# Moving a bias from TensorE into the PSUM eviction, and the eviction from ScalarE to VectorE

## The chip, the cores and the metric

The kernel runs on one NeuronCore of a Trainium2 chip. The metric is the device time of one execution in microseconds. The time before is the median of three runs.

## The reference

`x` has 8 batches of 256 tokens of 1024 features, fp32. Two residual layers follow each other:

```
x1  = x  + L0_ffn(quantize(x))            # 8 threshold groups, 64 levels; router, top 2 of 4 experts of rank 16
c   = x1 @ W.T + x1 @ lora_A[label[b]] @ lora_B_w.T * 0.5
out = x1 + c @ kernel + bias + low-rank terms of c (16 gated LoRAs of rank 32, one shared)
```

`bias` has 1024 elements, one for each output column, the same for every token and batch.

## The kernel before, in words

The kernel first folds the second layer's matrices into one 1024 x 1024 product P = I + W.T (kernel + shared LoRA), split into `p_hi` and `p_lo` for fp32r matmuls, and per-batch low-rank factors. That takes until about 206 us. The output loop follows, and meanwhile (from the start of the kernel on) the quantization of `x` runs on ScalarE and VectorE, batch after batch, because its result goes to TensorE for the router and the experts.

**The output loop on TensorE** (L945 to L987) has 64 steps q, eight for each batch b (j is the step in the batch). Each output tile n is 128 tokens by 512 columns, there are four for each batch, and a tile takes two steps, q = 2n and 2n + 1. A tile starts with the bias, as a matmul of a matrix of ones with a tile `bias` whose row 0 holds the bias rounded to fp32r and whose row 32 holds what the rounding left (L963). In each step 12 matmuls follow (L965 to L967, four slices of 128 features, three products each), and the tile ends with `close`, a matmul of the low-rank parts `zt` and `tb` (L942). `CLOSE[b]` is the earliest step at which tiles of batch b can be closed, since `zt` must be ready. Tiles use six PSUM banks in turn (`cols`). Besides, TensorE has in fixed steps: `mid(c)` (L848, 32 short matmuls of the quantized batch c with router and expert matrices), which waits for `q_made`; `gated_turn(c)` (L858); `z_begin(c)` (L870, L874) and `z_end(c)` (L881).

**ScalarE** evicts a finished tile from its bank to `ost` (`out_tile`, L480) at step TAKE[n], which is LAG = 3 steps behind the tile's close. SP then stores both halves of a 128-token block. Between these, ScalarE computes for each quantization group g of batch c `level` (L395), `val` (L406) and, once per batch, `absx` (L387); then `x_hi` (L455), `zt` (L446 and L571), `bu` (L462) and `expo` (L440). It works on the group of the step after its own.

**VectorE** takes for each group `val` (L598, waits for ScalarE), a mask `inside` (L608) and a merge (L615), and at the end of each batch L620, which signals `q_made`. A group takes some 5 us. Then `x_lo` (L707), and after each `mid(c)` eight small operations (`order(c)`, from L679, waits for `mid_made`) and five more (`gate(c)`, from L695).

**What sets the order.** Every engine's queue is written out by hand. The groups are spread over steps by the list TAKEN; `GROUPS[16 + q]` are those of step q. The last groups of the batches are in these steps: batch 3 in q = 11, batch 4 in 23, batch 5 in 34, batch 6 in 45, batch 7 in 56. `mid` follows in the steps 13, 25, 36, 46 and 57, `gated_turn` in 17, 29, 40, 49 and 60, `z_end` for batches 1 to 7 at the ends of the steps 7, 15, 23, 31, 41, 50 and 61. Group (3,5) is in q = 9, (4,3) in 17, (5,1) in 25, (5,5) in 31, (5,6) in 33. `order(6)` is in q = 47.

Of the kernel before, what the change touches and what calls it, by code (L numbers as in the profile page):

```python
# [26 lines left out]
F32 = mybir.dt.float32  # L27
# [8 lines left out]
P = 128  # L36
BATCH = 8
# [26 lines left out]
def build(nc, a, out_t, itok):  # L64
    arena = [(nc.sbuf_base + 31) // 32 * 32]

    def place(name, shape, dt, at=None, after=0):

        size = int(np.prod(shape[1:])) * mybir.dt.size(dt)
        size = (size + 31) // 32 * 32  # L70
        if at is None:
            at = arena[0]
            arena[0] += size
        t = nc.alloc_sbuf_tensor_at(name, shape, dt, offset=at + after)
        return t[:], at
# [24 lines left out]
    mg, _ = place("mg", [P, TT, 2 * ER], F32)  # L100
    zt, zt_at = place("zt", [P, ZSLOTS, TOK], F32)
    ident, _ = place("ident", [P, P], F32R)
    ones, _ = place("ones", [P, P], F32R)
    small, _ = place("small", [P, 3 * G + BATCH + RG], F32)
    par = small[:, 0:3 * G].rearrange("p (a g) -> p a g", a=3)
    gate_rep, gsel = small[:, 3 * G:3 * G + BATCH], small[:, 3 * G + BATCH:]
# [22 lines left out]
    alt, _ = place("alt", [P, BATCH // BG, D], F32, p_lo_at, half_bytes + KT * BATCH * R * 4)  # L129
    kp_hi, _ = place("kp_hi", [P, KT, HALF], F32R, x_hi_at)  # L130
    kp_lo, _ = place("kp_lo", [P, KT, HALF], F32R, x_lo_at)
    bias_raw, _ = place("bias_raw", [P, D], F32, ab_at)
    bias, _ = place("bias", [P, D], F32R, ab_at, D * 4)
    w_bytes = KT * P * 4
    w_hi = [place(f"w_hi{i}", [P, KT, P], F32R, xs_at, 2 * i * w_bytes)[0] for i in range(2)]
    w_lo = [place(f"w_lo{i}", [P, KT, P], F32R, xs_at, (2 * i + 1) * w_bytes)[0] for i in range(2)]
# [26 lines left out]
    xq_in = [sem("xq_in0"), sem("xq_in1")]  # L163
    k2_in, w_in, bet_in = sem("k2_in"), [sem("w_in0"), sem("w_in1")], sem("bet_in")
    bias_in, x_done = sem("bias_in"), sem("x_done")
    ones_made, bias_hi_made, bias_made, taken = sem("ones_made"), sem("bias_hi_made"), sem("bias_made"), sem("taken")
    lora_in = [sem(f"lora_in{g}") for g in range(NG)]
    small_in, warm_made = sem("small_in"), sem("warm_made")
    k_part_in = [sem(f"k_part_in{i}") for i in range(KPARTS)]
# [83 lines left out]

    ZEND = [max(b * KT - 1, OUT_AT[b] - STEPS) for b in range(BATCH)]
    CLOSE = [max(b * KT + 1, ZEND[b] + 1) for b in range(BATCH)]
    LAG = 3
    TAKE = [max(2 * q + 1, CLOSE[q // TILES]) + LAG for q in range(BATCH * TILES)]

    def slot(b, j):
        return STEPS + b * KT + j  # L260
# [12 lines left out]
    with nc.allow_non_contiguous_dma(reason="rows of 1 KB and small constants"), nc.Block() as block:  # L273
# [16 lines left out]
        def _(sp):  # L290
# [41 lines left out]
            for m in range(2, LOADS):  # L332
                n = step_of(m)
                sp.wait_ge(w_hi_made, former(m) + 1)
                sp.wait_ge(w_lo_made, former(m) + 1)
                sp.wait_ge(ufull, min(former(m) + 1, KT))
                sp.dma_start(wst[side(n)], w_v[tile_of(n)]).then_inc(w_in[side(n)], 16)
                if m - 2 < KT:
                    u_store(m - 2)
                if m == KT + 2:  # L340

                    for s in range(2):
                        sp.wait_ge(t_stored[s], 16 * NG // 2)
                    sp.wait_ge(kfull, HALVES * KT)
                    sp.wait_ge(v_made, HALVES)
                    for s in range(2):
                        sp.dma_start(tb[R:2 * R, s], tst[3 * R:4 * R, 0]).then_inc(v_moved, 16)
                        rows(s)
                    sp.dma_start(bias_raw, a["bias"]).then_inc(bias_in, 16)
            for s in range(2):  # L350
                sp.wait_ge(u_stored[s], 16 * KT // 2)
            sp.wait_ge(w_hi_made, LOADS - 1)
# [17 lines left out]
            for b in range(BATCH):  # L370
                if b + 2 < BATCH:
                    xs_load(b + 2)
                for t in range(TT):
                    sp.wait_ge(taken, b * TILES + (t + 1) * HALVES)
                    sp.dma_start(out_t[b, t], ost[:, t]).then_inc(out_stored[t], 16)
                if b + 2 < BATCH:
                    sp.wait_ge(ofull, STEPS + (b + 1) * TILES)
                    rows(b + 2)
# [4 lines left out]
        def _(act):  # L383
# [84 lines left out]
                    act.wait_ge(v_moved, 32)  # L468
                    nc.scalar.activation(tb[2 * R:P, s, h * HALF:(h + 1) * HALF], sbank[h][ER:2 * ER], ACT.Copy).then_inc(bp_made, 1)

            def bias_hi():
                act.wait_ge(bias_in, 16)
                nc.scalar.activation(bias, bias_raw, ACT.Copy).then_inc(bias_hi_made, 1)

            def out_tile(n):
                c, (t, h) = n // TILES, divmod(n % TILES, HALVES)
                act.wait_ge(ofull, STEPS + n + 1)
                if c:
                    act.wait_ge(out_stored[t], 16 * c)
                nc.scalar.activation(ost[:, t, h * HALF:(h + 1) * HALF], cols[n % CRING], ACT.Copy).then_inc(taken, 1)  # L480

            def rows_out(n):

                g, h = divmod(n, HALVES)
# [42 lines left out]
            for n in range(STEPS):  # L527

                if n == KT:
                    kp_split(1)  # L530
                if n and n + 1 < STEPS and n + 1 not in (KT, KT + 1):
                    weight_hi(load_of(n + 1))
                if n < KT:
                    act.wait_ge(ufull, n + 1)
                    if n >= 2:
                        act.wait_ge(u_stored[n % 2], 16 * (n // 2))
                    nc.scalar.activation(ust[:, n % 2], ubank, ACT.Copy).then_inc(u_made, 1)  # L537
                if n:
                    p_out(n - 1)
                if n == KT:  # L540
                    v_rows(1)
                if n == STEPS - 1:
                    act.wait_ge(ofull, STEPS - 1)
                    act.wait_ge(bet_in, 16)
                    nc.scalar.activation(bet_hi, bet, ACT.Copy).then_inc(bet_hi_made, 1)
                if n in OUT:
                    gated_out(OUT[n])
                if n == STEPS - 2:
                    bias_hi()

                for c, g in GROUPS[n + 1]:
                    quant(c, g)
                if n in RANK:
                    gate_exp(RANK[n])
# [6 lines left out]
                quant(c, g)  # L561
            bp_out(0)
            bu_out(0)
            for q in range(BATCH * KT + LAG + 1):
                b, j = divmod(q, KT)
                if q - 1 in ZEND:
                    z = ZEND.index(q - 1)
                    act.wait_ge(zfull, z + 1)
                    if z >= ZSLOTS:
                        act.wait_ge(ofull, STEPS + (z - ZSLOTS + 1) * TILES)  # L570
                    nc.scalar.activation(zt[0:2 * R, z % ZSLOTS], zbank[0:2 * R, 0:TOK], ACT.Copy).then_inc(zt_made, 1)  # L571
                if q == 1:
                    bp_out(1)
                for n in range(BATCH * TILES):
                    if TAKE[n] == q:
                        out_tile(n)
                if slot(b, j) in OUT:
                    gated_out(OUT[slot(b, j)])
                if 0 < q < BATCH * KT:
                    for c, g in GROUPS[slot(b, j) + 1]:  # L580
                        quant(c, g)
                if slot(b, j) in RANK:
                    gate_exp(RANK[slot(b, j)])
                if b + 1 < BATCH and j in XAT:
                    x_part(b + 1, XAT.index(j))
                if b + 1 < BATCH and j == ZAT:
                    bu_out(b + 1)
            for n in range(BATCH * TILES):
                if TAKE[n] > BATCH * KT + LAG:
                    out_tile(n)  # L590

        @block.vector
        def _(dve):
# [59 lines left out]


            nc.vector.memset(warm, 1.0).then_inc(warm_made, 1)
            nc.vector.memset(ones.bitcast(F32), 1.0).then_inc(ones_made, 1)
            dve.wait_ge(small_in, 16)
            nc.vector.max(thr, par[:, 0])
            nc.vector.reciprocal(inv, par[:, 1])
# [104 lines left out]
            p_out(STEPS - 1)  # L764
            for p in range(XPARTS):
                x_part(0, p)
            dve.wait_ge(bias_hi_made, 1)
            nc.vector.tensor_tensor(bias[R:2 * R], bias_raw[R:2 * R], bias[R:2 * R].bitcast(F32),
                                    ALU.subtract).then_inc(bias_made, 1)
            for b in range(BATCH):  # L770
                for j in range(KT):
                    ranks(slot(b, j))
                    for c, g in GROUPS[slot(b, j)]:
                        quant(c, g)
                    if b + 1 < BATCH and j - 1 in XAT:
                        x_part(b + 1, XAT.index(j - 1))

        @block.tensor
        def _(pe):
# [165 lines left out]
            for q in range(BATCH * KT):  # L945
# [5 lines left out]
                if part == 0:  # L951
                    if n < RING:
                        pe.wait_ge(ofree, STEPS)
                    elif n < CRING:
                        pe.wait_ge(bp_made, 2 * HALVES)
                    else:
                        pe.wait_ge(taken, n - CRING + 1)
                o, at = cols[n % CRING], slice(t * P, (t + 1) * P)
                if part == 0:
                    if n == 0:  # L960
                        pe.wait_ge(ones_made, 1)
                        pe.wait_ge(bias_made, 1)
                    mm(o, ones, bias[:, h * HALF:(h + 1) * HALF], start=True, stop=False)  # L963
                for k in range(part * KT // 2, (part + 1) * KT // 2):
                    mm(o, x_hi[:, s, k, at], p_hi[:, h, k], start=False, stop=False)  # L965
                    mm(o, x_hi[:, s, k, at], p_lo[:, h, k], start=False, stop=False)  # L966
                    last = mm(o, x_lo[:, s, k, at], p_hi[:, h, k], start=False, stop=False)  # L967
                if j == KT - 1:
# [57 lines left out]
```

## Time and profile before

| | |
|---|---|
| median of 3 runs | 488.93 us (487.65 to 489.24) |
| profiled execution, its own time | 489.24 us |
| its span | 487.5 us |
| PE busy | 471.8 us, 97% |
| VectorE busy | 391.4 us, 80% |
| ScalarE busy | 356.6 us, 73% |

The span runs from the first to the last instruction of the profiled execution, and the execution's own time has a little around it. Engines are named PE (TensorE), DVE (VectorE), ACT (ScalarE), SP and POOL. Matmuls are pipelined, and the duration of one in the profile is longer than the distance to the next; a busy PE is thus not PE at its peak. An engine's instructions overlap their neighbours a little as well, so the distance from start to start is what an instruction takes from its queue. PEclk is TensorE's granted clock, 1.00 for 2.4 GHz and 0.50 for 1.2 GHz.

### The profile page before, as it was taken

The numbers are of one execution on the slowest core, as the hardware profiler recorded it, in microseconds if no ns is written. First come the engines' busy times: TensorE is split into PE (matmuls) and PEld (weight loads), VectorE is DVE, ScalarE is ACT, GpSimd is POOL, SyncE is SP. The second block draws the span as 40 slices with busy tenths as digits, with TensorE's granted clock in tenths as the row PEclk, the third lists the DMA queues.
The fourth block names the chain that finished last, engine by engine and source line by source line (L and its number), as shares of the span: only waits on it lengthen the run. The fifth ranks groups of instructions, "written<-read, shape, count | busy, mean of one in ns | idle before, by whom it ended". The sixth has DMA issues, their size and how long they took to land.

```text
span 487.5 us, 5645 instructions
## 1 busy us (share of the span) xinstructions
PE 471.8 (97%) x2200; PEld 365.7 (75%) x2200; DVE 391.4 (80%) x381; ACT 356.6 (73%) x297; POOL 6.8 (1%) x12
## 2 busy tenths in 40 slices
PE   6989999999889999999999999999999999999896
PEld 5963788887648888787777777787787768767774
DVE  3289978789979989939879989798799994999400
ACT  3779987864978398676699599776899697776001
POOL 0000000001000001000000000000000000000000
PEclk9599999999999999999999999999999999999799
DMA  8975542313301527030441316014214013102002
GB/s 281 422 267 178 171 142 73 90 43 98 107 0 37 181 86 204 13 108 1 151 141 44 108 54 200 38 55 130 108 54 152 0 55 129 56 0 86 1 0 87
DMA packets 35500, 50.61 MB, mean 104 GB/s; under 512 B 26610, under 2 KB 26866, under 8 KB 33074
## 3 DMA queue, kind: packets, MB, share of 16 engines
q1 hardware_dynamic: 34322, 41.87, 26.7%
q0 software_dynamic: 1152, 8.39, 4.8%
q8 instruction: 17, 0.28, 0.2%
q14 instruction: 9, 0.07, 0.1%
HBM read 39.51 MB, written 10.49 MB: 103 GB/s over the span
## 4 chain that ended last, share of the span: by engine, by line
PE 76%; DVE 16%; issue 4%; DMA 2%; ACT 1%; SPq 0%; DVEq 0%; ACTq 0%
PE bank L965 10%; PE bank L966 10%; PE bank L967 10%; DVE val L615 7%; PE bank L848 6%; PE bank L942 5%; PE bank L874 5%; PE bank L917 5%; PE bank L913 5%; PE bank L914 4%; PE bank L896 3%; DVE inside L608 3%; PE bank L814 3%; DVE val L598 2%; DMA la<-la_in 2%
## 5 line engine op out<-in xcount | busy, mean ns | idle before, releaser
L406 ACT ACTIVATE val<-level,shift,small 128x2048 f32<-128x2048 int16 x64 | 133.8, 2091 | 16.3 <-DVE val L615 16.2
L615 DVE COPY_PREDICATED val<-inside,val 128x2048 f32<-128x2048 uint8 x56 | 141.3, 2523 | 0.3
L395 ACT ACTIVATE level<-xq,inv 128x2048 int16<-128x2048 f32 x64 | 127.9, 1998 | 2.0 <-DMA xq<-xt_in 1.4
L598 DVE TENSOR_SCALAR val<-val,width,unshift 128x2048 f32<-128x2048 f32 x64 | 86.0, 1347 | 22.7 <-ACT val L406 22.4
L965 PE MATMUL bank<-p_hi,x_hi 128*128 128x512 f32 x256 | 102.5, 401 | 0.0
L966 PE MATMUL bank<-p_lo,x_hi 128*128 128x512 f32 x256 | 100.4, 392 | 0.0
L967 PE MATMUL bank<-p_hi,x_lo 128*128 128x512 f32 x256 | 100.4, 392 | 0.0
L608 DVE TENSOR_SCALAR inside<-absx,thr 128x2048 uint8<-128x2048 f32 x56 | 71.4, 1285 | 7.1 <-ACT absx L387 7.1
L965 PEld LDWEIGHTS bank<-p_hi,x_hi 128*128 128x128 f32 x256 | 48.5, 189 | 17.6 <-issue 8.8
L966 PEld LDWEIGHTS bank<-p_lo,x_hi 128*128 128x128 f32 x256 | 48.4, 189 | 10.5 <-issue 0.5
L967 PEld LDWEIGHTS bank<-p_hi,x_lo 128*128 128x128 f32 x256 | 48.3, 189 | 10.5
L913 PE MATMUL bank<-kp_hi,w_hi 128*128 128x512 f32 x128 | 50.8, 397 | 1.8 <-DVE kp_lo L652 1.8
L917 PE MATMUL bank<-kp_hi,w_lo 128*128 128x512 f32 x128 | 50.4, 393 | 0.0
L914 PE MATMUL bank<-kp_lo,w_hi 128*128 128x512 f32 x128 | 49.9, 390 | 0.0
L848 PEld LDWEIGHTS bank<-ra,val 128*128 128x128 f32 x256 | 31.5, 202 | 3.0 <-DVE val L620 1.7
L848 PE MATMUL bank<-ra,val 128*128 128x68 f32 x256 | 31.5, 284 | 1.3 <-DVE val L620 1.3
L942 PE MATMUL bank<-tb,zt 128*128 128x512 f32 x64 | 32.7, 599 | 0.0
L896 PE MATMUL bank<-aefft,wst 128*128 128x256 f32 x128 | 29.1, 380 | 2.2 <-ACT ust L537 2.2
L874 PE MATMUL bank<-xs,ub 128*64 128x256 f32 x128 | 29.3, 382 | 0.0
L896 PEld LDWEIGHTS bank<-aefft,wst 128*128 128x128 f32 x128 | 24.1, 190 | 6.9 <-issue 3.4
L913 PEld LDWEIGHTS bank<-kp_hi,w_hi 128*128 128x128 f32 x128 | 24.1, 188 | 6.3 <-issue 2.0
L917 PEld LDWEIGHTS bank<-kp_hi,w_lo 128*128 128x128 f32 x128 | 24.0, 188 | 5.2
(91 smaller groups left out, 477.4 us busy)
## 6 DMA issues: line engine op xcount, KB each, us to landing
xq<-xt_in POOLq DMA_DIRECT2D x8, 1024.0 KB, 5.8
xs<-xt_in SPq DMA_DIRECT2D x8, 1024.0 KB, 4.9
out_t<-ost SPq DMA_DIRECT2D x16, 512.0 KB, 3.0
wst<-w_in SPq DMA_DIRECT2D x14, 512.0 KB, 3.6
la<-la_in SPq DMA_DIRECT2D x4, 512.0 KB, 10.4
kst<-k_in SPq DMA_DIRECT2D x4, 512.0 KB, 13.9
lb<-lb_in SPq DMA_DIRECT2D x1, 2048.0 KB, 18.7
kst<-k_in SPq DMA_DIRECT2D x1, 2048.0 KB, 7.9
```

Source lines behind the costliest of these rows:

```text
L395: nc.scalar.activation(level[:, g % 2], xq[:, c % 2], ACT.Copy, scale=inv[:, g:g + 1]).then_inc(levels_made, 1)
L406: nc.scalar.activation(val[:, turn(c, g)], level[:, g % 2], ACT.Relu, bias=shift[:, g:g + 1], scale=par[:, 1, g:g + 1]).then_inc(raised, 1)
L598: nc.vector.tensor_scalar(v, v, width[:, g:g + 1], unshift[:, g:g + 1], ALU.min, ALU.add).then_inc(valued, 1)
L608: nc.vector.tensor_scalar(inside[:, g % 2], absx, thr[:, g - 1:g], None, ALU.is_le).then_inc(masked, 1)
L615: nc.vector.copy_predicated(val[:, acc(c)], inside[:, g % 2], val[:, turn(c, g)]).then_inc(merged, 1)
L848: last = mm(midbank[:, t * RT:(t + 1) * RT], val[:, acc(c), k, t * P:(t + 1) * P], ra[:, k], start=k == 0, stop=k == KT - 1)
L913: mm(obank[n % RING], w_hi[side(n)][:, o], kp_hi[:, o], start=o == 0, stop=False)
L914: mm(obank[n % RING], w_hi[side(n)][:, o], kp_lo[:, o], start=False, stop=False)
L917: last = mm(obank[n % RING], w_lo[side(n)][:, o], kp_hi[:, o], start=False, stop=o == KT - 1)
L965: mm(o, x_hi[:, s, k, at], p_hi[:, h, k], start=False, stop=False)
L966: mm(o, x_hi[:, s, k, at], p_lo[:, h, k], start=False, stop=False)
L967: last = mm(o, x_lo[:, s, k, at], p_hi[:, h, k], start=False, stop=False)
```

## The change

The bias matmul goes, with the ones matrix and the bias's rounding and remainder. `bias` now holds the bias in all 128 rows as fp32, loaded by the same DMA. The eviction is done by VectorE as an addition of the bank and the bias, at the steps TAKE with LAG = 2 instead of 3, ahead of the step's other work. It waits for the tile's close, for the bias's load, and for the store that frees `ost`; it signals `ofree` where ScalarE signalled `taken`, and TensorE (for the bank) and SP (for the store) wait for that. With LAG 2 the tiles 0, 1, 2, ... 19 are taken in q = 3, 5, 7, ... 41, tiles 20 to 23 in q = 44, 45, 47 and 49, 24 and 25 in 53, 26 in 55, 27 in 57, and the last four behind the loop. The first matmul of a tile now starts the accumulation.

```diff
-    ones, _ = place("ones", [P, P], F32R)
-    bias_raw, _ = place("bias_raw", [P, D], F32, ab_at)
-    bias, _ = place("bias", [P, D], F32R, ab_at, D * 4)
+    bias, _ = place("bias", [P, D], F32, ab_at)
...
-    LAG = 3
+    LAG = 2
     TAKE = [max(2 * q + 1, CLOSE[q // TILES]) + LAG for q in range(BATCH * TILES)]
...
-                    sp.dma_start(bias_raw, a["bias"]).then_inc(bias_in, 16)
+                    sp.dma_start(bias, a["bias"]).then_inc(bias_in, 16)
...
-                    sp.wait_ge(taken, b * TILES + (t + 1) * HALVES)
+                    sp.wait_ge(ofree, STEPS + b * TILES + (t + 1) * HALVES)
...
-            def bias_hi():
-                act.wait_ge(bias_in, 16)
-                nc.scalar.activation(bias, bias_raw, ACT.Copy).then_inc(bias_hi_made, 1)
-
-            def out_tile(n):
-                c, (t, h) = n // TILES, divmod(n % TILES, HALVES)
-                act.wait_ge(ofull, STEPS + n + 1)
-                if c:
-                    act.wait_ge(out_stored[t], 16 * c)
-                nc.scalar.activation(ost[:, t, h * HALF:(h + 1) * HALF], cols[n % CRING], ACT.Copy).then_inc(taken, 1)
...
-            nc.vector.memset(ones.bitcast(F32), 1.0).then_inc(ones_made, 1)
...
-            dve.wait_ge(bias_hi_made, 1)
-            nc.vector.tensor_tensor(bias[R:2 * R], bias_raw[R:2 * R], bias[R:2 * R].bitcast(F32),
-                                    ALU.subtract).then_inc(bias_made, 1)
+            def out_tile(n):
+                c, (t, h) = n // TILES, divmod(n % TILES, HALVES)
+                dve.wait_ge(ofull, STEPS + n + 1)
+                dve.wait_ge(bias_in, 16)
+                if c:
+                    dve.wait_ge(out_stored[t], 16 * c)
+                half = slice(h * HALF, (h + 1) * HALF)
+                nc.vector.tensor_tensor(ost[:, t, half], cols[n % CRING], bias[:, half], ALU.add).then_inc(ofree, 1)
+
             for b in range(BATCH):
                 for j in range(KT):
+                    for n in range(BATCH * TILES):
+                        if TAKE[n] == b * KT + j:
+                            out_tile(n)
                     ranks(slot(b, j))
...
+            for n in range(BATCH * TILES):
+                if TAKE[n] >= BATCH * KT:
+                    out_tile(n)
...
-                        pe.wait_ge(taken, n - CRING + 1)
+                        pe.wait_ge(ofree, STEPS + n - CRING + 1)
                 o, at = cols[n % CRING], slice(t * P, (t + 1) * P)
-                if part == 0:
-                    if n == 0:
-                        pe.wait_ge(ones_made, 1)
-                        pe.wait_ge(bias_made, 1)
-                    mm(o, ones, bias[:, h * HALF:(h + 1) * HALF], start=True, stop=False)
                 for k in range(part * KT // 2, (part + 1) * KT // 2):
-                    mm(o, x_hi[:, s, k, at], p_hi[:, h, k], start=False, stop=False)
+                    mm(o, x_hi[:, s, k, at], p_hi[:, h, k], start=k == 0, stop=False)
...
-        "bias": c(np.where((i16 % P == 0)[:, None] | (i16 == R)[:, None], v["L1_ffn_bias"][None, :], np.float32(0))),
+        "bias": c(np.broadcast_to(v["L1_ffn_bias"], (P, D))),
```

## Rows read from the trace of the kernel before

**Rows 1.** The page's first part: busy us, share of the span, instructions.
```profile
PE 471.8 (97%) x2200; PEld 365.7 (75%) x2200; DVE 391.4 (80%) x381; ACT 356.6 (73%) x297; POOL 6.8 (1%) x12
```
**Rows 2.** Busy time by stretch; columns in the first line.
```profile
core 0: us, PE busy (x) PEld busy (x) DVE busy (x) ACT busy (x) POOL busy (x), PEclk, DMA share, GB/s
136.00:150.00 14.00, 12.18 (x47) 8.28 (x46) 11.47 (x14) 12.48 (x15) 0.00 (x0) 1.00 0.00 1
206.00:456.00 250.00, 248.71 (x1212) 188.87 (x1210) 218.26 (x195) 196.46 (x150) 1.59 (x3) 1.00 0.25 81
456.00:463.20 7.20, 7.20 (x31) 6.62 (x31) 2.24 (x13) 0.21 (x1) 0.00 (x0) 0.53 0.01 2
```
**Rows 3.** VectorE's waits from 206 to 456 us: total, times, longest.
```profile
DVE val L598 <- ACT val L406: 16.7, 7, 4.6
DVE lg L679 <- PE bank L848: 5.8, 1, 5.8
DVE x_lo L707 <- ACT x_hi L455: 4.3, 1, 4.3
DVE inside L608 <- ACT absx L387: 1.4, 3, 0.5
```
**Rows 4.** VectorE in order of time: start, duration, operation [idle before it <-releaser].
```profile
246.66 1.35 DVE L598 TENSOR_SCALAR val<-val,width,unshift 128x2048 f32<-128x2048 f32 x1 [4.55 <-ACT val L406]
...
281.81 1.35 DVE L598 TENSOR_SCALAR val<-val,width,unshift 128x2048 f32<-128x2048 f32 x1 [1.88 <-ACT val L406]
...
313.83 1.35 DVE L598 TENSOR_SCALAR val<-val,width,unshift 128x2048 f32<-128x2048 f32 x1 [2.79 <-ACT val L406]
...
342.81 1.35 DVE L598 TENSOR_SCALAR val<-val,width,unshift 128x2048 f32<-128x2048 f32 x1 [2.71 <-ACT val L406]
...
349.40 1.35 DVE L598 TENSOR_SCALAR val<-val,width,unshift 128x2048 f32<-128x2048 f32 x1 [1.54 <-ACT val L406]
...
403.94 2.35 DVE L620 SCALAR_TENSOR_TENSOR val<-absx,thr,val 128x2048 f32<-128x2048 f32 x1
412.13 0.17 DVE L679 COPY lg<-bank 128x8 f32<-128x8 f32 x1 [5.84 <-PE bank L848]
...
452.43 2.35 DVE L620 SCALAR_TENSOR_TENSOR val<-absx,thr,val 128x2048 f32<-128x2048 f32 x1
```
**Rows 5.** TensorE in order of time, around `mid` 6 and `mid` 7.
```profile
408.41 3.68 PE L848 MATMUL bank<-ra,val 128*128 128x68 f32 x32
...
453.16 0.39 PE L967 MATMUL bank<-p_hi,x_lo 128*128 128x512 f32 x1
454.84 5.71 PE L848 MATMUL bank<-ra,val 128*128 128x68 f32 x32 [1.29 <-DVE val L620]
...
467.44 0.40 PE L963 MATMUL bank<-bias,ones 128*128 128x512 f32 x1
467.68 0.39 PE L965 MATMUL bank<-p_hi,x_hi 128*128 128x512 f32 x1
```
**Rows 6.** Groups of instructions: busy us, mean ns of one, idle before.
```profile
L963 PE MATMUL bank<-bias,ones 128*128 128x512 f32 x32 | 22.6, 706 | 0.0
L480 ACT ACTIVATE ost<-bank 128x512 f32<-128x512 f32 x32 | 18.6, 587 | 8.8 <-PE bank L942 8.6
L647 DVE TENSOR_TENSOR kst<-bank,kst 128x512 f32<-128x512 f32 x16 | 10.4, 676 | 0.0
```
**Rows 7.** ScalarE in order of time, around two evictions.
```profile
242.16 0.58 ACT L480 ACTIVATE ost<-bank 128x512 f32<-128x512 f32 x1
242.64 1.99 ACT L395 ACTIVATE level<-xq,inv 128x2048 int16<-128x2048 f32 x1
...
483.75 0.60 ACT L480 ACTIVATE ost<-bank 128x512 f32<-128x512 f32 x1 [3.00 <-PE bank L942]
```
**Rows 8.** VectorE in order of time, an addition of this form and its successor.
```profile
62.43 0.68 DVE L647 TENSOR_TENSOR kst<-bank,kst 128x512 f32<-128x512 f32 x1
63.02 1.22 DVE L639 TENSOR_TENSOR w_lo<-wst,w_hi 128x1024 fp32r<-128x1024 f32 x1
```
**Rows 9.** TensorE in order of time, an earlier wait.
```profile
142.84 0.47 PE L913 MATMUL bank<-kp_hi,w_hi 128*128 128x512 f32 x1 [1.82 <-DVE kp_lo L652]
```

More of the change, by code:

```diff
@@ L165, in build @@
     bias_in, x_done = sem("bias_in"), sem("x_done")
-    ones_made, bias_hi_made, bias_made, taken = sem("ones_made"), sem("bias_hi_made"), sem("bias_made"), sem("taken")
     lora_in = [sem(f"lora_in{g}") for g in range(NG)]
@@ L547, in _ @@
                     gated_out(OUT[n])
-                if n == STEPS - 2:
-                    bias_hi()
                 for c, g in GROUPS[n + 1]:
@@ L563, in _ @@
             bu_out(0)
-            for q in range(BATCH * KT + LAG + 1):
+            for q in range(BATCH * KT + LAG):
                 b, j = divmod(q, KT)
@@ L573, in _ @@
                     bp_out(1)
-                for n in range(BATCH * TILES):
-                    if TAKE[n] == q:
-                        out_tile(n)
                 if slot(b, j) in OUT:
@@ L587, in _ @@
                     bu_out(b + 1)
-            for n in range(BATCH * TILES):
-                if TAKE[n] > BATCH * KT + LAG:
-                    out_tile(n)
         @block.vector
```

## The prediction

> **What bounds the kernel now.** I read the busy times first: TensorE is busy for 97% of the span, VectorE for 80%, ScalarE for 73% [rows 1]. By that row TensorE is the bound, and time taken from it should come back. The table by stretch says more. From 206 to 456 us (nearly all of the output loop) TensorE is busy 248.7 of 250 us and VectorE 218.3 [rows 2], so VectorE has 31.7 us to spare, and its waits say where: 16.7 us in seven waits for ScalarE's `val`, 4.3 for `x_hi`, 5.8 for the product `mid` of batch 6 [rows 3]. The order of time shows the rest: after 412.13 VectorE does not pause until its last quantization operation ends at 454.78 (452.43 plus 2.35), and TensorE, which came to the product `mid` of batch 7 at 453.55, waits 1.29 us for it [rows 4, 5]. So two engines are nearly level at 454.8 us: the end is set there by VectorE, and then by 32.7 us (487.5 less 454.8) of TensorE work that hardly anything can shorten.
>
> Two things about that wait matter. TensorE's clock is granted in full over the whole loop, but 0.53 in the mean from 456 to 463.2 us [rows 2], which is almost all of it at the lower level, 1.2 GHz of 2.4. And the 32 matmuls of `mid` (batch 7) take 5.71 us, where those of batch 6, which TensorE began without a wait, take 3.68 [rows 5]. A pause of 1.29 us was followed by some 7 us at half clock.
>
> **What the change removes.** (a) On TensorE, 32 bias matmuls (L963). Their listed mean of 706 ns [rows 6] is a modelled end; the cost is start to start, 467.44 to 467.68, 0.24 us [rows 5]. 32 x 0.24 is 7.7 us, the first of the tail, which falls into the half clock, twice that, 0.48. (b) On ScalarE, 32 evictions of 587 ns [rows 6], each followed by the next instruction 0.48 us later (242.16 to 242.64 [rows 7]), about 15.4 us, and one copy of the bias. (c) On VectorE, one subtraction of the bias, ahead of its 4.3 us wait for `x_hi` [rows 3], which takes up whatever it gives: nothing. The bias copy on ScalarE stands two steps ahead of the loop, and the `x_hi` of batch 0 behind it waits for a load that SP issues only when TensorE has ended the last product of the stage before (line 359): nothing too. The bias DMA keeps its 512 KB.
>
> **What it adds.** 32 additions of a PSUM bank and an SBUF row block on VectorE. The trace has exactly this form at L647, 676 ns [rows 6]. What VectorE's queue loses is again start to start: 62.43 to 63.02, rounded up 0.60 us [rows 8]. I take 0.60. The other end is 0.68, the listed time, if the overlap with the neighbours doesn't come about; below 0.59 nothing in the trace points. VectorE is where the trace has least room, so each tile is followed through its order. By the new take steps (LAG 2), tiles 0 to 3 stand ahead of group (3,5), 4 to 7 ahead of (4,3), 8 to 11 ahead of (5,1), 12 to 14 ahead of (5,5), 15 ahead of (5,6), 16 to 21 ahead of the end of batch 6, 22 in the wait for `mid` 6, 23 to 26 ahead of the end of batch 7, and 27 to 31 behind it, where VectorE idles.
>
> The Trainium skill, "VectorE: DVE Perf Modes", section on the TRN2 errata, gives an fp32 tensor_tensor of N elements (N+151)/0.96 ns, 691 ns here, and holds that the latency is exposed between instructions, once for each, so that many small ones pay it each time. The durations of the trace agree with it, the pitch of 0.60 does not; by the page the 22 tiles that count below would cost 2.0 us more, which by itself would turn the -1.0 of the walk below into a loss.
>
> **The walk along VectorE**, as shift against before. At the waits for `val` ScalarE comes from a TensorE event (the end of z, or the gated transpose), which moves forward by 0.24 us for each bias matmul ahead of it, plus 0.48 for an eviction no longer in ScalarE's way [rows 7].
> - (3,5) at 246.66, behind 4.55 us of idle [rows 4]: the tiles fit into the idle; ScalarE is earlier by 4 x 0.24 + 0.48. Shift -1.4.
> - (4,3) at 281.81, idle 1.88: -1.4 - 1.88 + 4 x 0.60 = -0.9. ScalarE would be ready at -(8 x 0.24 + 0.48) = -2.4, so VectorE's own work is now last.
> - (5,1) at 313.83, idle 2.79: -0.9 - 2.79 + 2.4 = -1.3; ScalarE -3.4.
> - (5,5) at 342.81, idle 2.71, and one of the three waits for `absx` on the way (1.4 us together [rows 3], 0.46 each): -1.3 - 3.17 + 1.8 = -2.7; ScalarE -3.6.
> - (5,6) at 349.40, idle 1.54: -2.7 - 1.54 + 0.6 = -3.6; ScalarE -4.3.
> - End of batch 6, 403.94 + 2.35 = 406.29, another wait for `absx` on the way: -3.6 - 0.46 + 6 x 0.60 = -0.45, so 405.85.
>
> TensorE would come to `mid` 6 at 408.41 less 24 x 0.24, at 402.7, and now waits until 405.9: 3.2 us. It ends at 409.5 instead of 412.1, and VectorE goes on 2.6 us earlier (its wait of 5.84 us becomes 3.6, and tile 22 lies in it). Then 42.7 us of unbroken work and 4 x 0.60: the end of batch 7 at 454.78 - 2.6 + 2.4 = 454.6. TensorE is there at 453.55 - 2.6 - 5 x 0.24 = 449.75 and waits 4.9 us instead of 1.29. In the tail three bias matmuls go (0.48 + 0.24 + 0.24, about 0.9) and the last eviction, at 483.75 for 0.60 [rows 7], costs 0.68 on VectorE, +0.1. Sum: -0.2 - 0.9 + 0.1 = -1.0 us. So of 7.7 us taken from TensorE some 6.7 turn into waits for VectorE.
>
> **The new waits.** Each addition waits for its tile's close two steps back. Queued behind it are the quantization groups, for which the `mid` products wait. VectorE runs level with TensorE or behind it from 281 us on, so the tile is closed by then; ahead of that the wait falls into idle. I cost it at nothing; where it isn't, a tile that comes up 1 us late costs 1 us. The stores now follow VectorE's semaphore; SP has no other work there, and the 512 KB store has two steps in hand. TensorE's wait for a bank is six tiles deep, nothing. x_lo of the next batch is ready four steps ahead, also nothing.
>
> **The clock.** The wait of 3.2 us ahead of `mid` 6 is new, and what follows it lies on VectorE's path. If the clock falls as it did at `mid` 7, that product takes 5.71 - 3.68 = 2.0 us more; if the fall comes after the product, nothing, since TensorE then has nearly 5 us in hand. There is evidence for both: a wait of 1.82 us at 142.84 [rows 9] was followed by no fall (granted 1.00 from 136 to 150 us [rows 2]), one of 1.29 was. The product itself ran on the second occasion, so that row is nearer, but where in the product the fall comes is open; I take half, +1.0. At `mid` 7 the fall is already paid for. The Trainium skill, "TensorE: Matmul & The Clock Gate", section "Why this matters for your kernels", warns that idle gaps between bursts of matmuls bring the half clock back; the trace agrees at `mid` 7, and by that rule alone, with both waits long, the sum would take the full 2.0 and come to +1.0.
>
> **Forecast.** -1.0 + 1.0 = 0.0 us. The profiled execution took 489.24 us around its span of 487.5, and it is the slowest of three, 0.31 above their median of 488.93. I put the shift onto the median: 488.9 us. What can be told from no change is about 0.3%, 1.5 us.
>
> **Rivals.**
> A. TensorE stays the bound: VectorE's 31.7 spare us hold the 27 tiles (16 us) that come before 456 us. Then all 32 matmuls' 7.7 us come back, perhaps with the fall of the clock: 481 to 482. For it: the spare time is twice what is added. Against: most of it lies before 350 us or in the wait on `mid` 6, while from 412 to 454.8 there is none. 15 in 100.
> B. Slower, VectorE's pace: the additions cost 0.68 us each, as listed, in the 22 places that count (22 x 0.08 = +1.8), and the half clock falls on `mid` 6 in full (+2.0): -1.0 + 3.8 = +2.8, 491.7 us. With the clock's fall it counts as slower from 0.62 us per tile, without it from 0.71. For it: the listed durations and the 1.29 us wait that was enough. Against: the pitch of 0.60 at the operation of the same form [rows 8]. 27 in 100.
> C. The new waits hold VectorE up behind unclosed tiles, or ScalarE's path is later than worked out, with 1 us here and there over six batches: +3 to +5, about 493. 5 in 100.
> The forecast's case has 53, within 487.0 to 490.9 by itself.
>
> **Chances.** Faster by over 0.3%: A and a small part of the forecast's case (no fall of the clock, and half a microsecond more absorbed), 0.22. Slower: B, C and a little of the forecast's case at its upper end, 0.34. The rest, 0.44, within 0.3%. The range of 485.3 to 492.6 takes in B and leaves out A and most of C.
>
> **What would show it.** No L963; TensorE's busy time down by some 20 us as listed (7.7 real); 32 VectorE additions of 0.68 us with 0.60 from start to start; no VectorE idle over 1 us between 250 and 405 us; TensorE waits of about 3 and 5 us ahead of the `mid` products at 406 and 454.6 us; ScalarE's waits longer. The step on the clock is right if the granted clock has a second dip after 403 us. I am wrong if VectorE still waits for `val` after 281 us (A), if the 27th tile's step ends well after 455 us (B), or if additions wait for TensorE (C).

## The result and the profile after

The changed kernel is slower: ratio 1.0068 (95% interval 1.0039 to 1.0099), with medians of 491.3 against 489.24 us in seven runs of each. The ratio is not the quotient of these two medians, which is 1.0042: in all there are 18 timed runs of the changed kernel, and their median is 492.07. Measured again in the second set of experiments, the ratio was 1.0053 (1.0026 to 1.0079). The forecast was no change. The profiled execution has a span of 490.6 us, 3.2 more than before.

The page's first part and the group of the additions, to set beside [rows 1] and [rows 6]:

```profile
PE 471.1 (96%) x2168; PEld 365.4 (74%) x2168; DVE 408.6 (83%) x411; ACT 339.7 (69%) x264; POOL 8.5 (2%) x12
```
```profile
L751 DVE TENSOR_TENSOR ost<-bank,bias 128x512 f32<-128x512 f32 x32 | 22.6, 713 | 17.7 <-PE bank L931 17.7
```

TensorE has lost 32 matmuls and hardly any busy time. The order of time says why. First VectorE, to set beside [rows 4] (start, duration, operation, idle before it):

```profile
245.31 1.35 DVE L576 TENSOR_SCALAR val<-val,width,unshift 128x2048 f32<-128x2048 f32 x1 [2.20 <-ACT val L403]
...
280.12 0.73 DVE L751 TENSOR_TENSOR ost<-bank,bias 128x512 f32<-128x512 f32 x1
280.71 1.39 DVE L576 TENSOR_SCALAR val<-val,width,unshift 128x2048 f32<-128x2048 f32 x1
...
312.41 1.33 DVE L576 TENSOR_SCALAR val<-val,width,unshift 128x2048 f32<-128x2048 f32 x1
...
339.74 1.34 DVE L576 TENSOR_SCALAR val<-val,width,unshift 128x2048 f32<-128x2048 f32 x1
...
402.81 2.35 DVE L598 SCALAR_TENSOR_TENSOR val<-absx,thr,val 128x2048 f32<-128x2048 f32 x1
405.08 0.68 DVE L751 TENSOR_TENSOR ost<-bank,bias 128x512 f32<-128x512 f32 x1
412.14 0.17 DVE L656 COPY lg<-bank 128x8 f32<-128x8 f32 x1 [6.38 <-PE bank L837]
...
454.83 2.35 DVE L598 SCALAR_TENSOR_TENSOR val<-absx,thr,val 128x2048 f32<-128x2048 f32 x1
```

Up to the end of batch 6 (402.81 plus 2.35 is 405.16) this is nearly the walk of the prediction: the waits for `val` are gone from 281 us on, and an addition takes 0.59 to 0.60 us from its queue (280.12 to 280.71). Then VectorE waits 6.4 us, and resumes at 412.14, which is where it resumed before. TensorE and its granted clock show what stands between, to be set beside [rows 5] and [rows 2]:

```profile
405.22 6.89 PE L837 MATMUL bank<-ra,val 128*128 128x68 f32 x32 [2.02 <-DVE val L598]
...
457.24 7.09 PE L837 MATMUL bank<-ra,val 128*128 128x68 f32 x32 [3.11 <-DVE val L598]
```
```profile
206.00:405.00 199.00, 197.20 (x961) 148.61 (x959) 186.94 (x178) 156.14 (x104) 3.92 (x3) 1.00 0.29 94
405.00:415.40 10.40, 10.18 (x40) 9.43 (x41) 3.71 (x14) 4.57 (x4) 0.00 (x0) 0.52 0.01 2
415.40:457.00 41.60, 38.72 (x173) 28.53 (x171) 41.46 (x31) 22.31 (x15) 0.00 (x0) 0.99 0.08 29
457.00:466.50 9.50, 9.27 (x38) 8.78 (x39) 2.60 (x13) 0.21 (x1) 0.00 (x0) 0.50 0.15 57
```

The clock (PEclk, third column from the right) stays at 1.00 until TensorE waits 2.02 us for VectorE, and is then at its lower level, 1.2 GHz, for about 10 us. `mid` 6 takes 6.89 us, 3.68 before. The second wait, 3.11 us, is followed by the same, and `mid` 7 takes 7.09 us, 5.71 before.

**Where the 3.2 us are**, from these rows: `mid` 6 starts 3.2 us earlier than before and lasts 3.2 longer, so it ends level with before. Four additions lie in VectorE's last stretch, 2.4 us. `mid` 7 lasts 1.4 longer. From its end to the last eviction it was 23.2 us before (460.55 to 483.75 [rows 7]) and is 22.5 now (464.33 to 486.82, the row below), since three bias matmuls are gone; the last eviction itself takes 0.1 longer. 0 + 2.4 + 1.4 - 0.7 + 0.1 = 3.2.

```profile
486.82 0.69 DVE L751 TENSOR_TENSOR ost<-bank,bias 128x512 f32<-128x512 f32 x1 [2.91 <-PE bank L931]
```

### The profile page after: what moved, and what is told of

Its sections match the earlier page's. It is cut to its first block, busy times and chain, and to the rows that moved or that the text cites. A ratio compares the mean times of both kernels' runs of the same rounds, so it can differ in the third digit from the quotient of the medians.

```text
span 490.6 us, 5581 instructions
## 1 busy us (share of the span) xinstructions
PE 471.1 (96%) x2168; PEld 365.4 (74%) x2168; DVE 408.6 (83%) x411; ACT 339.7 (69%) x264; POOL 8.5 (2%) x12
## 4 chain that ended last, share of the span: by engine, by line
PE 62%; DVE 26%; issue 7%; DMA 2%; ACT 2%; SPq 0%; DVEq 0%; ACTq 0%
DVE val L593 12%; PE bank L949 7%; PE bank L951 7%; PE bank L950 7%; PE bank L837 6%; DVE val L576 5%; PE bank L906 5%; PE bank L902 5%; PE bank L903 4%; PE bank L931 3%; PE bank L863 3%; DVE inside L586 3%; PE bank L885 3%; PE bank L803 3%; DMA la<-la_in 2%
## 5 line engine op out<-in xcount | busy, mean ns | idle before, releaser
L403 ACT ACTIVATE val<-level,shift,small 128x2048 f32<-128x2048 int16 x64 | 133.8, 2090 | 22.5 <-DVE val L593 22.4
L949 PE MATMUL bank<-p_hi,x_hi 128*128 128x512 f32 x256 | 113.1, 442 | 0.0
L837 PEld LDWEIGHTS bank<-ra,val 128*128 128x128 f32 x256 | 35.9, 226 | 7.2 <-DVE val L598 6.0
L837 PE MATMUL bank<-ra,val 128*128 128x68 f32 x256 | 36.1, 310 | 5.1 <-DVE val L598 5.1
L751 DVE TENSOR_TENSOR ost<-bank,bias 128x512 f32<-128x512 f32 x32 | 22.6, 713 | 17.7 <-PE bank L931 17.7
```

What stands on the lines that cost most here:

```text
L403: nc.scalar.activation(val[:, turn(c, g)], level[:, g % 2], ACT.Relu, bias=shift[:, g:g + 1], scale=par[:, 1, g:g + 1]).then_inc(raised, 1)
L837: last = mm(midbank[:, t * RT:(t + 1) * RT], val[:, acc(c), k, t * P:(t + 1) * P], ra[:, k], start=k == 0, stop=k == KT - 1)
L949: mm(o, x_hi[:, s, k, at], p_hi[:, h, k], start=k == 0, stop=False)
```

## The experiments

The theory: the additions make VectorE the last engine, TensorE waits for it where it hadn't waited, or had waited less, and each such wait is followed by half clock, which doubles the time of the very product that VectorE waits for. The rival: VectorE's added work makes it slower by itself, and the clock is a symptom. All timed runs stand against runs of the kernel before from the same set and chip; ratios have 95% intervals. The first four kernels were one set, the next four another, both on the chip numbered 15, and the last two a third, on chip 4. The medians of the kernel before were 490.46, 489.05 and 490.2 us in the three sets, so ratios of different sets are compared with care.

One thing matters where the spans of single profiled executions are compared. The output loop's first matmul starts at 206.94 us in the profile before and at 206.97 in that of the changed kernel, but anywhere from 206.5 to 208.3 in the others; why it varies isn't shown. Where this matters, spans are given from the loop's start.

**Filling the waits of the changed kernel.** Filler matmuls are put into TensorE's waits; their results are not used. They go into a bank that the next tile overwrites.

```diff
                 if slot(b, j) in MID:
+                    filler = {6: 8, 7: 20}.get(MID[slot(b, j)], 0)
+                    if filler:
+                        pe.wait_ge(ofree, STEPS + n + 1 - CRING + 1)
+                    for i in range(filler):
+                        mm(cols[(n + 1) % CRING], p_hi[:, 0, i % KT, 0:P], p_hi[:, 0, i % KT], start=True, stop=True)
                     mid(MID[slot(b, j)])
```

> The changed kernel with filler matmuls of 512 columns on TensorE, into the bank that the next tile overwrites anyway: 8 ahead of mid 6 (1.8 us at 0.227) and 20 ahead of mid 7 (4.5 us). They fill the two waits for VectorE and change nothing else. Clock theory (the waits of 2.0 and 3.1 us let the clock fall, and half-speed mid products are what makes the change slower): the clock stays at 1.00 until the tail, mid 6 takes 3.7 us instead of 6.9, mid 7 3.7 instead of 7.1, the end of batch 7 on VectorE comes at about 454.0 instead of 457.2, and the span falls by 3.2 (mid 6) and about 4.7 (mid 7 and the matmuls behind it), from 490.6 to about 483. Rival (VectorE's added work alone makes it slower, the clock is only a symptom): no change, 490 to 491, or slower by what the filler overruns.

Measured: 485.83 us against 490.46, ratio 0.9916 (0.9889 to 0.9942), span 482.9. TensorE does more work and the kernel is faster. Its two `mid` products, with TensorE's remaining waits (the granted clock is 1.00 from 206 to 480 us):

```profile
405.15 3.79 PE L837 MATMUL bank<-ra,val 128*128 128x68 f32 x32 [0.39 <-DVE val L598]
...
454.06 3.79 PE L837 MATMUL bank<-ra,val 128*128 128x68 f32 x32 [0.27 <-DVE val L598]
```

VectorE delivers batch 6 at the same time as without filler. The rest follows from the two products of 3.79 us (3.1 and 3.3 us less) and from the matmuls behind `mid` 7, which no longer run at half clock. The rival in its simple form is out: at an unchanged amount of VectorE's work the slowdown turns into a gain.

**The same in the kernel before**, with five fillers.

```diff
+                    filler = {7: 5}.get(MID[slot(b, j)], 0)
+                    if filler:
+                        pe.wait_ge(taken, n + 1 - CRING + 1)
+                    for i in range(filler):
+                        mm(cols[(n + 1) % CRING], p_hi[:, 0, i % KT, 0:P], p_hi[:, 0, i % KT], start=True, stop=True)
```

> The kernel before with 5 filler matmuls (1.1 us) in TensorE's wait of 1.29 us ahead of mid 7. Clock theory: no fall at 456 us, mid 7 takes 3.7 instead of 5.7 us, and the matmuls behind it run at full rate: 3.4 us less, a span of about 484. Rival: no change, since the wait itself stays.

Measured: 486.42 us, ratio 0.9941 (0.9913 to 0.9969), span 484.8, `mid` 7:

```profile
455.41 3.79 PE L848 MATMUL bank<-ra,val 128*128 128x68 f32 x32
```

As the theory had it: from the loop's start (207.60 us here) the span is 3.4 us shorter than before, as expected. With the clock up in both, the change is worth 485.83 against 486.42, -0.6 us, which the intervals don't separate from nothing. The profiled executions, counted from the loop's start (206.72 and 207.60 us), give 276.2 against 277.2 us, and that is the walk's -1.0.

**`mid` of the last two batches one step later**, first on the changed kernel and then on the one before.

```diff
-    LAGS = [(2, 3, 4, 5, 6)] * 2 + [(2, 4, 5, 6, 7)] * (BATCH - 4) + [(1, 2, 3, 4, 5)] * 2
+    LAGS = [(2, 3, 4, 5, 6)] * 2 + [(2, 4, 5, 6, 7)] * (BATCH - 4) + [(2, 3, 4, 5, 6)] * 2
```

> The changed kernel with mid and what follows from it one step later for batches 6 and 7, so that TensorE has a step's 12 matmuls (2.7 us) to do in place of its waits. Clock theory: at mid 6 (wait 2.0 us in the changed kernel) no wait and no fall; VectorE does tile 22 and the first operation of group (7,0) meanwhile and resumes some 2.5 us earlier; the end of batch 7 at about 453.6; a wait of about 3 us at most remains at mid 7, perhaps with a fall. Span 481 to 485. Rival (VectorE's added work alone): only what VectorE wins by the new order, 1 to 2 us, so 488 to 490.

> The kernel before with the same move of mid for batches 6 and 7. Clock theory: TensorE no longer waits at mid 7 (1.29 us), and its clock doesn't fall: 1.3 + 3.4 = 4.7 us less, about 483. Rival: the wait alone goes, 1.3 us, about 486, less still if a fourth close at the end costs.

Measured on the changed kernel: 486.33 us, ratio 0.9931 (0.9904 to 0.9957). The profiled execution, at 481.41 us the fastest of its thirteen, had no fall of the clock, although TensorE waited 1.25 us at `mid` 7:

```profile
406.16 3.68 PE L837 MATMUL bank<-ra,val 128*128 128x68 f32 x32
...
453.55 3.79 PE L837 MATMUL bank<-ra,val 128*128 128x68 f32 x32 [1.25 <-DVE val L598]
```

Its other twelve runs lie between 484.9 and 487.5, some 3.5 to 6 us above. They have no profile, but each run has its mean granted clock: 0.986 in the profiled one, 0.971 to 0.979 in the twelve. A stretch of 10 us at half clock, as behind `mid` 6 above, lowers the mean of 485 us by 0.010 (an estimate from these rows), so the twelve have about one such stretch more. Where it lay isn't shown.

On the kernel before it was a miss: 487.47 us, ratio 0.9954 (0.9924 to 0.9983), 485.7 of span where 483 was expected. The wait and the fall at `mid` 7 are gone, as expected. In the profiled execution 1.3 us of the difference lie ahead of the output loop, which starts at 208.20 us. The rest I put down to `mid` 6: TensorE had not waited for it before, and moving it costs VectorE a longer wait, 8.19 us instead of 5.84:

```profile
416.98 0.17 DVE L679 COPY lg<-bank 128x8 f32<-128x8 f32 x1 [8.19 <-PE bank L848]
```

**The two halves of the change alone.** First the bias matmuls taken out of the kernel before (the bias is then missing in the output):

```diff
-                    mm(o, ones, bias[:, h * HALF:(h + 1) * HALF], start=True, stop=False)
...
-                    mm(o, x_hi[:, s, k, at], p_hi[:, h, k], start=False, stop=False)
+                    mm(o, x_hi[:, s, k, at], p_hi[:, h, k], start=k == 0, stop=False)
```

> The kernel before without the 32 bias matmuls; eviction stays on ScalarE. The bias is left out of the output. It shows what TensorE's side of the change is worth alone. By the walk along VectorE its waits for ScalarE shrink with TensorE's events, the end of batch 6 comes at about 402.4, mid 6 5.8 us earlier without a wait, the end of batch 7 at 449, a wait of 2.5 us there: 6.7 us less in all, less 1 for a deeper fall of the clock: a span of 481 to 482, ratio 0.987. Rival (the bias matmuls lay beside VectorE's work and are worth nothing on the path): 486 or more.

Measured: 485.98 us against 489.05, ratio 0.9924 (0.9892 to 0.9956), span 484.2. The direction is right; of the forecast's 1.3% the median shows 0.8. In the profiled execution the walk holds better than its span of 484.2 says. Its loop starts 1.4 us later than before. The granted clock was lower over the first 45 us (0.81 against 0.85) and from 100 to 136 us (0.95 against 1.00), but that alone isn't the cause: the execution with seven more additions, below, has the same figures and a loop that starts at 206.98 us. The loops' first matmuls, before and here:

```profile
206.94 0.50 PE L963 MATMUL bank<-bias,ones 128*128 128x512 f32 x1
```
```profile
208.31 0.50 PE L964 MATMUL bank<-p_hi,x_hi 128*128 128x512 f32 x1
```

Counted from there, `mid` 6 starts 5.4 us earlier than before (5.8 expected), and the whole is 4.7 us shorter. At `mid` 7 the wait was 2.60 us, twice that of before, and the product took the full 7.09:

```profile
450.98 7.09 PE L848 MATMUL bank<-ra,val 128*128 128x68 f32 x32 [2.60 <-DVE val L620]
```

Then the move of the eviction alone; the bias matmuls stay, and the edits to the waits are those of the change:

```diff
-    LAG = 3
+    LAG = 2
...
-                nc.scalar.activation(ost[:, t, h * HALF:(h + 1) * HALF], cols[n % CRING], ACT.Copy).then_inc(taken, 1)
+                nc.vector.tensor_copy(ost[:, t, half], cols[n % CRING]).then_inc(ofree, 1)
```

> The bias matmuls stay on TensorE, and VectorE evicts by a copy in place of ScalarE, at the changed kernel's steps. VectorE's side of the change alone. By the walk: end of batch 6 at about 405.9, TensorE comes to mid 6 at 408.4 as before, without a wait and without a fall; end of batch 7 at 454.8 + 2.4 = 457.2; a wait of 3.7 us instead of 1.3 there with a full fall of the clock (mid 7 7 us instead of 5.7). Span 487.5 + 2.4 + 1.3 = 491.2, ratio 1.008. Rival (moving the eviction costs nothing, ScalarE's relief pays for it): 487 to 488.

Measured: 493.84 us, ratio 1.0095 (1.0062 to 1.0128), span 492.9. The loop again starts 1.3 us late, at 208.28 us; counted from there the whole is 4.1 us longer than before, where 3.7 was expected. The waits are about those walked, 0.19 us (none expected) without a fall and 3.65 us (3.7) with one:

```profile
410.10 3.79 PE L849 MATMUL bank<-ra,val 128*128 128x68 f32 x32 [0.19 <-DVE val L607]
...
459.00 7.10 PE L849 MATMUL bank<-ra,val 128*128 128x68 f32 x32 [3.65 <-DVE val L607]
```

One step of that expectation was wrong: VectorE ended batch 6 at 410.05 us (407.70 plus 2.35) and not at 405.9, and so level with TensorE. The 405.9 was the changed kernel's; with the bias matmuls in place TensorE's events come no earlier, and VectorE still waits for ScalarE's `val` late in the loop:

```profile
344.15 1.35 DVE L585 TENSOR_SCALAR val<-val,width,unshift 128x2048 f32<-128x2048 f32 x1 [1.59 <-ACT val L406]
...
407.70 2.35 DVE L607 SCALAR_TENSOR_TENSOR val<-absx,thr,val 128x2048 f32<-128x2048 f32 x1
```

So the halves are -0.8% and +0.9%. The matmuls do lie on the path, and the evictions on VectorE cost about as much. The two halves don't add up to the change: from the loop's start the profiled executions give -4.7 and +4.1 us, together -0.6, and the changed kernel has +3.1. In neither half does TensorE wait more than 0.2 us at `mid` 6, and in neither does the clock fall there; with both it waits 2.0 us, the clock falls, and the product takes 3.2 us more. (These are single executions; the ratios alone, within their intervals, don't show that the halves fail to add up.)

**The changed kernel again**, in the same set.

> The changed kernel itself, on this chip beside the others, to have its ratio again: about 1.007 of the kernel before, by every theory. The clock theory adds that its fastest runs stay well above the fastest of the kernel before, because both of its waits (2.0 and 3.1 us) let the clock fall in every run, while the wait of 1.3 us of the kernel before lets it fall in most.

Measured: 1.0053, as given above; its fastest of twelve runs was 490.72, against 485.12 for the fastest of 24 of the kernel before. The profiled execution waited 2.15 and 2.63 us and had both falls, the first of them later within the product, so that `mid` 6 took only 4.82 us:

```profile
405.65 4.82 PE L837 MATMUL bank<-ra,val 128*128 128x68 f32 x32 [2.15 <-DVE val L598]
...
455.57 6.76 PE L837 MATMUL bank<-ra,val 128*128 128x68 f32 x32 [2.63 <-DVE val L598]
```

**A wait at `mid` 6 without the change.** Nothing of bias or eviction is touched; VectorE gets seven additions more, whose results are not used:

```diff
+                    if slot(b, j) in (STEPS + 37, STEPS + 39, STEPS + 41):
+                        for i in range(3 if slot(b, j) == STEPS + 41 else 2):
+                            nc.vector.tensor_tensor(bias_raw[:, 0:HALF], bias_raw[:, HALF:D], bias_raw[:, HALF:D], ALU.add).then_inc(pad_step, 1)
+                            pads[0] += 1
+                            dve.wait_ge(pad_step, pads[0])
```

> The kernel before with 7 additions of 512 columns on VectorE (5.0 us, results unused) ahead of the end of batch 6, so that TensorE waits for VectorE at mid 6 as in the changed kernel, by some 2.6 us; bias and eviction are as before. It asks whether a wait there is enough for the clock to fall. Clock theory: mid 6 takes 6.9 us instead of 3.7, and the time rises by 2.6 + 3.2 = 5.8 us, ratio 1.012. Rival (the fall comes from what the change does to TensorE's own stream): mid 6 takes 3.7 us, and the time rises by 2.6 us alone, ratio 1.005.

Measured: 493.33 us against 490.2, ratio 1.0077 (1.0045 to 1.0109).

```profile
411.03 6.88 PE L854 MATMUL bank<-ra,val 128*128 128x68 f32 x32 [2.42 <-DVE val L620]
...
462.24 3.79 PE L854 MATMUL bank<-ra,val 128*128 128x68 f32 x32 [1.13 <-DVE val L620]
```

A wait of 2.42 us, made by VectorE alone, is followed by the fall, and the product takes 6.88 us instead of 3.68; nothing in TensorE's own stream is different. The time rose by less than expected (3.1 us and not 5.8), and the second row shows why in part: at `mid` 7, with a wait of 1.13 us, the clock didn't fall this time, where [rows 5] has a fall behind 1.29.

**Late evictions.** Tiles 24 to 26 are taken behind the end of batch 7.

```diff
+    TAKE[24:27] = [57] * 3
```

> The changed kernel with the tiles 24 to 26 taken behind the end of batch 7 alone; mid stays where it was. VectorE's path loses 3 x 0.60 = 1.8 us: end of batch 7 at 455.4, the waits stay (2.0 us, and 1.3 instead of 3.1), and so do both falls of the clock. Clock theory: 1.8 us less than the changed kernel, ratio 1.003. Rival (the additions inside VectorE's last stretch cost nothing): ratio 1.007.

Measured: 488.94 us, ratio 0.9992 (0.9966 to 1.0019). The changed kernel's 1.0053 and 1.0068 lie 3 to 4 us above, so the additions in the last stretch do cost something; with intervals of some 0.3% on each ratio, the expected 1.8 us isn't excluded. The profiled execution was the slowest of its thirteen (492.57), with 2.09 and 1.58 us of waits and both falls. Its loop started at 208.26 us, 1.3 later than that of the changed kernel, and from there `mid` 7 starts 1.4 us earlier than in it (248.8 against 250.3 us), near the 1.8 expected.

**Both together**, `mid` later and late evictions.

> The changed kernel with mid of the batches 6 and 7 one step later, and with the tiles 24 to 26 taken only behind the end of batch 7 (step 57), where VectorE waits for mid 7 anyway. The end of batch 7 comes 3 x 0.60 = 1.8 us earlier than in the version with mid later alone (453.4), at 451.6, before TensorE is there (452.3). So no wait is left at either mid, and the clock stays up in every run: span about 478.3, time about 480, ratio 0.979 to 0.982. Rival (with mid later, the remaining time isn't set by VectorE): 486, as the median of that version.

Measured: 480.56 us against 489.05, ratio 0.9811 (0.9771 to 0.9851), all six runs between 479.83 and 481.26, a smaller spread than any other kernel here has, with the fewest runs. TensorE comes to both products without a wait, and the granted clock from 206 us to the end of both is 1.00:

```profile
407.27 3.68 PE L838 MATMUL bank<-ra,val 128*128 128x68 f32 x32
...
453.28 3.68 PE L838 MATMUL bank<-ra,val 128*128 128x68 f32 x32
```
```profile
206.00:457.00 251.00, 248.43 (x1221) 188.69 (x1220) 233.51 (x224) 182.99 (x122) 3.90 (x3) 1.00 0.25 80
```

The late tiles lie where VectorE has nothing else to do, four additions in a row in 2.48 us:

```profile
452.78 2.48 DVE L752 TENSOR_TENSOR ost<-bank,bias 128x512 f32<-128x512 f32 x4
```

## Why the prediction was wrong

- **VectorE becomes the last engine.** Right. The walk put the end of batch 6 at 405.85; it came at 405.16 (402.81 plus 2.35). Of its stations, (3,5) was at 245.31 (walk 245.3), (4,3) at 280.71 (280.9), (5,1) at 312.41 (312.5), (5,5) at 339.74 (340.1).
- **The price of an addition.** Right: 0.60 us from start to start, 713 ns as listed. The rule of the Trainium skill that I weighed ("VectorE: DVE Perf Modes", the section on the errata) gives the listed duration about right, 691 ns; as a charge on the queue it would have been too high here.
- **The new waits of the additions.** Right for the stretch that counts. The 17.7 us that L751 waited lie behind the last `mid`, where VectorE is idle anyway.
- **TensorE's waits.** Sizes 3.2 and 4.9 us were forecast, 2.0 and 3.1 measured. The second was shorter since TensorE had itself lost time at half clock after the first.
- **The clock.** This is the step that failed, by its size. The prediction had 0 or +2.0 us at `mid` 6, took half, +1.0, and had "At `mid` 7 the fall is already paid for". Measured: +3.2 at `mid` 6 and +1.4 at `mid` 7, together 4.6 where 1.0 was forecast. Two things were wrong in it. The upper end came from the product of 5.71 us, which in the profile before ran its first 1.5 us at full clock, as the two stretches below show; a product that is slow nearly throughout takes 6.9 to 7.1 us, so the price is then 3.2 to 3.4, not 2.0. And "already paid" overlooked that a fall has a size, which depends on when it comes: at `mid` 7 of the changed kernel the granted clock is 0.50 from 456.8 us on, and the product begins at 457.24.

```profile
454.84:456.20 1.36, 1.36 (x12) 1.36 (x13) 0.00 (x0) 0.00 (x0) 0.00 (x0) 1.00 0.00 0
456.40:460.50 4.10, 4.10 (x21) 4.10 (x21) 0.00 (x0) 0.00 (x0) 0.00 (x0) 0.50 0.01 4
```

- **Half of the 2.0** was taken because both the fall and its place in the product were uncertain. The doubt about the fall rested on a wait of 1.82 us without one [rows 9]. The runs with a profile have now 12 waits of over 1 us at these products. All eight from 2.02 to 3.65 us had a fall; of the four from 1.13 to 1.58, two (1.29 and 1.58). Of those eight, seven cost 3.1 to 3.4 us in the product and one (2.15 us, 4.82 in place of 3.68) only 1.1. On these runs a wait of over 2 us is to be priced nearly in full. The Trainium skill's "TensorE: Matmul & The Clock Gate", section "Why this matters for your kernels", named the risk, and the sum by it, +1.0, was on the right side and too small, as it used my 2.0. The gaps that it warns of are longer than 1.29 us, though, so the fall at `mid` 7 in the profile before bears it out in kind and not in length.
- **The sum.** With 3.2 at `mid` 6 and 1.4 at `mid` 7 in place of 1.0, the walk's -1.0 becomes +3.6, against 3.2 of span measured. The median of 491.3 us lies inside the range of 485.3 to 492.6, but on the slower side, where the forecast had no change.
- **The rivals.** B forecast 491.7 us by a price of 0.68 per addition and half clock at `mid` 6. The time came close partly by luck: the first of its two mechanisms did not occur, and its place was taken by the larger clock term. A and C are refuted: TensorE waits for VectorE at both products, and VectorE doesn't wait for closes ahead of 457 us.

## What to carry to other kernels

Where two engines arrive nearly level, moving work from one to the other moves the wait, and a wait of TensorE has a second price: here 2 us of waiting brought 3.2 us more in the product that the other engine was waiting for. Price that product as slow throughout, unless a trace shows when the fall comes. Before the work is moved, look for what TensorE could do in the wait and for what the other engine could do behind its last delivery; here these two reorderings, one line each, turned a loss of 0.5% into a gain of 1.9% in the same set. Part of it isn't the change's: the later `mid` alone gave the kernel before 0.5%.

## What the runs showed of the hardware

- Filler matmuls in a wait paid for themselves here: 28 of them, some 6.4 us of added TensorE work, made the changed kernel some 1.4 to 1.5% faster (0.9916 against 1.0053 and 1.0068, from different sets).
- The lower clock is not tied to a wait's length alone. 1.13 and 1.25 us brought no fall, 1.29 did, and after 2.15 us the fall came late enough that `mid` 6 took 4.82 us instead of 6.9. The same kernel's runs differ by over 5 us: 34 of the kernel before in the first set lie between 486.1 and 491.8, with one cluster at 486.1 to 486.7 and the largest at 490.1 to 490.7. That it is the fall at `mid` 7 which parts them isn't shown; the time at which the output loop starts alone differs by 1.8 us between the profiled executions.
- An addition with a PSUM operand and a PSUM eviction of 128x512 fp32 take 0.60 us of VectorE's queue, against 0.48 of ScalarE's [rows 7].
